# First attention stage of a two-layer network: whole masks behind the products of the maxima, and the maxima's sign on GpSimd

## The chip, the core and the metric

The kernel runs on one core of a Trainium2 chip. A core has a matrix engine (TensorE, PE in the rows; its weight loads are listed apart, as PEld), a vector engine (VectorE, DVE), an activation engine (ScalarE, ACT), GpSimd (POOL), and a queue engine (SyncE, SP) that starts the transfers here. The metric is the time of one execution in microseconds (us), the median of several. Before the change it is 1973.1 us (three runs, 1972.66 to 1973.49).

## The reference, cut to what matters

The network adds four blocks to a residual stream of 4 sequences of 1024 tokens and 128 features. Only the first block is touched. Per sequence and head (16 heads of 8 features, so 64 pairs of head and sequence):

```
q, k, v = (layernorm(x) @ W.T + b) split into 16 heads of 8
sim     = q @ k.T + bias[bucket(i - j)] * SCALE     # bias by distance, per head
sim     = sim - inf where key j > query i           # causal
attn    = softmax(sim);  out = attn @ v
x       = x + out @ Wo.T + bo
```

Later blocks are a tree-routed feed-forward attention, a second attention with 16 heads (unmasked softmax, then masked) and a gated feed-forward layer.

## The kernel before, in words

The stage is `attend_causal`. It has 64 steps, one for each pair of head and sequence, and each engine runs its own list of instructions, written out by hand; semaphores tie the lists together. Queries and keys lie in HBM as three bf16 parts each, from which 48 rows are made (6 pairs of parts by 8 features), loaded twice: into partitions 0 to 47 and 64 to 111. So a product can use the upper or the lower half of TensorE's 128 rows, and products on different halves run side by side. "Half" below always means this half of the rows.

What a step n does:

- **Maxima.** For each block of 128 queries (8 blocks, qb) TensorE makes the causal part of `q k` (128 by (qb+1)·128 elements) in PSUM, as bf16. The blocks are grouped in five tiles, `MAXIMA = [(7,), (0, 6), (1, 5), (2, 4), (3,)]`, called T0 to T4 below, which take turns in two buffers `psM` of two PSUM banks each. The columns of bank 0 come from half 0, those of bank 1 from half 1. The last 128 columns of each block are the diagonal; `mask` (L703) adds minus 1e30 above it with two products of 64 rows each, on the half that wrote them (identity rows times a table). VectorE takes each block's row maxima (L627), then makes minus the maxima as two bf16 parts, high and low (L637, L639).
- **Rows.** One product with an identity (L741, 128 rows, 16 columns) turns these parts into rows; ScalarE copies them (L674) and two transfers put them behind the 48 rows of `qS` (L514), so that a later product also subtracts the maximum.
- **Scores.** Nine units of 512 columns, called u0 to u8 (`PIECES`), each with keys on the partitions; each runs on one half, the two halves in turn, and writes to one of three banks in turn (`psS`). ScalarE takes each with an exponential (L694) to `probs`. u0 waits for the rows' transfer. GpSimd multiplies the columns near the diagonal by the bias factor (L663), eight multiplications a step.
- **Values.** 26 f32 products of `probs` with values and ones (L777, L781), 128 rows by 32 columns, four column groups side by side; each has two records. They come in three parts, `VALUES[0]` to `VALUES[2]`, called V0 to V2.

TensorE's list for a step, with work of three steps in it: u0, u1 of n; T0, T1 of n+2; u2, u3; V0 of n-1; the rows product L741 of n+1; u4; T2; u5, u6; T3; V1; u7, u8; T4; V2. Scores run for n, maxima for n+2, values for n-1.

V0 waits for all eight GpSimd multiplications of step n-1. GpSimd's list is: the eight multiplications of a step, then the copy of the next values (L655).

Of the kernel before, what the change touches and what calls it, by code (L numbers as in the profile page):

```python
# [18 lines left out]
ALU = mybir.AluOpType  # L19
ACT = mybir.ActivationFunctionType  # L20
AXX = mybir.AxisListType.X
# [3 lines left out]
P = 128  # L25
B = 4
# [5 lines left out]
TPB = T // P  # L32
CH = 512
# [23 lines left out]
HALF = 64  # L57
PROWS = PAIRS * HD
# [462 lines left out]
def attend_causal(nc, m, g):  # L521


    NG = HEADS * B
# [4 lines left out]
    ORDER = [0, 1, 2, 3, ROWS, 4, 5, 6, 7, 8]  # L529
    MAXIMA = [(7,), (0, 6), (1, 5), (2, 4), (3,)]  # L530
    NM = len(MAXIMA)
    NEAR_ORDER = [0, 1, 7, 2, 6, 3, 5, 4]
    NEAR_AFTER = [0, 2, 3, 4, 5, 6, 7, 8]
    VALUES = [[(0, 0), (1, 0), (2, 0), (3, 0), (0, 1), (1, 1), (2, 1), (3, 1), (0, 2), (1, 2), (2, 3), (3, 4), (0, 3)],
              [(0, 4), (1, 3), (2, 2), (3, 2), (0, 5), (1, 4)],
              [(0, 6), (1, 5), (2, 4), (3, 3), (0, 7), (1, 6), (2, 5)]]

    ENDS = VALUES[2][-4:]

    def place(kb, qb):  # L540

        for unit, pieces in enumerate(PIECES):
            at = unit * CH
            for of, first, count in pieces:
                if of == kb and first <= qb * P < first + count:
                    return at + qb * P - first
                at += count
        raise AssertionError((kb, qb))

    def near_width(kb):  # L550
# [12 lines left out]
    psO = m.ps("psO", [P, CH])  # L563
    ring = Ring(ORDER, NG, psS)
# [5 lines left out]
    maxima_done, max_taken, block_taken = m.sem("maxima_done"), m.sem("max_taken"), m.sem("block_taken")  # L570
    nm_hi, nm_ready = m.sem("nm_hi"), m.sem("nm_ready")
    slot_done, slot_taken = m.sem("slot_done"), m.sem("slot_taken")
    near_done, v_staged = m.sem("near_done"), m.sem("v_staged")
    pv_done, o_taken = m.sem("pv_done"), m.sem("o_taken")

    with nc.Block() as block:
# [36 lines left out]
        @block.vector  # L613
        def _(dve):
            for u in range(BUFS):
                dve.memset(kS[u][:, :], 1.0).then_inc(cleared, 1)
            for n in range(NG):
                p = n % 2
                for i, blocks in enumerate(MAXIMA):
                    dve.wait_ge(maxima_done, n * NM + i + 1)  # L620
                    at = 0
                    for qb in blocks:
                        if i == 0 and n >= 2:

                            dve.wait_ge(nm_ready, n - 1)
                        w = (qb + 1) * P
                        last = dve.tensor_reduce(mx[:, p, qb:qb + 1], psM[(n * NM + i) % 2][:, at:at + w], AXX, ALU.max)  # L627
                        if qb != blocks[-1]:
                            last.then_inc(block_taken, 1)
                        at += w  # L630
                    last.then_inc(max_taken, 1)
                dve.wait_ge(max_taken, (n + 1) * NM)
                dve.wait_ge(block_taken, (n + 1) * (TPB - NM))
                if n >= 2:

                    dve.wait_ge(slot_done, ring.rows(n - 2) + 1)
                dve.tensor_scalar(nm[:, p, 0, :], mx[:, p, :], -1.0, None, ALU.mult).then_inc(nm_hi, 1)  # L637
                dve.wait_ge(nm_hi, n + 1)
                dve.scalar_tensor_tensor(nm[:, p, 1, :], mx[:, p, :], -1.0, nm[:, p, 0, :], ALU.mult, ALU.subtract).then_inc(nm_ready, 1)  # L639

        @block.gpsimd
        def _(pool):
            for v in v_ones:
                pool.memset(v[:, :, :], 0.0).then_inc(pool_ready, 1)
            pool.wait_ge(pool_ready, len(v_ones))
            for v in v_ones:
                pool.memset(v[:, :, HD:2 * HD], 1.0).then_inc(pool_ready, 1)
            pool.wait_ge(pool_ready, 2 * len(v_ones))

            def stage_v(n):  # L650
                if n >= 3:

                    pool.wait_ge(pv_done, n - 2)
                src = g["v_all"][:, :, :, :].rearrange("p h (b t) e -> p (h b) t e", b=B)[:, n, :, :]
                pool.tensor_copy(v_ones[n % 3][:, :, 0:HD], src).then_inc(v_staged, 1)  # L655

            stage_v(0)
            for n in range(NG):
                pr = probs[n % 2]
                for kb, unit in zip(NEAR_ORDER, NEAR_AFTER):  # L660
                    pool.wait_ge(slot_taken, ring.index(n, unit) + 1)
                    a, w = place(kb, kb), near_width(kb)
                    pool.tensor_tensor(pr[:, a:a + w], pr[:, a:a + w], g["ebias"][:, n // B, 0:w], ALU.mult).then_inc(near_done, 1)  # L663
                if n + 1 < NG:
                    stage_v(n + 1)

# [34 lines left out]
        def _(pe):  # L701
            def mask(out, r, table):

                for s in range(2):
                    done = pe.matmul(out, g["masks"][r:r + HALF, s, 0, :], g["masks"][r:r + HALF, s, table, :], start=False, stop=s == 1)  # L705
                return done

            def maxima(n, i):

                if n >= NG:  # L710
                    return
                u, k = n % BUFS, n * NM + i
                if k >= 2:

                    pe.wait_ge(max_taken, k - 1)
                if i == 0:
                    pe.wait_ge(s_loaded[u], (n // BUFS + 1) * 64)
                ps = psM[k % 2]
                at = 0
                for qb in MAXIMA[i]:  # L720
                    w = (qb + 1) * P
                    for bank in range(2):
                        a, z = max(at, bank * CH), min(at + w, (bank + 1) * CH)
                        if a >= z:
                            continue
                        r, ends = HALF * bank, z == at + w
                        last = pe.matmul(ps[:, a:z], qS[u][r:r + PROWS, qb * P:(qb + 1) * P], kS[u][r:r + PROWS, a - at:z - at], start=True, stop=not ends)  # L727
                        if ends:
                            last = mask(ps[:, z - P:z], r, 1)
                    at += w  # L730
                last.then_inc(maxima_done, 1)

            def rows(n):
# [28 lines left out]
            def values(n, part):  # L762

                if n < 0:
                    return
                if part == 0:
                    pe.wait_ge(v_staged, n + 1)
                    pe.wait_ge(near_done, (n + 1) * TPB)
                    if n > 0:
                        pe.wait_ge(o_taken, n)  # L770
                pr, v = probs[n % 2][:, :], v_ones[n % 3]
                for c, kb in VALUES[part]:
                    out = psO[c * VW:(c + 1) * VW, 0:2 * P]
# [1052 lines left out]
def build(nc, ins, out, phases=99):  # L1826
    ctx = ExitStack()
    with ctx:
# [92 lines left out]
```

## Time and profile before

| | |
|---|---|
| median of three runs | 1973.1 us |
| profiled execution: its time, its span | 1974.91 us, 1973.2 us |
| busy over the whole span: PE, DVE, ACT, POOL | 85%, 80%, 63%, 38% |
| VectorE's maxima in this stage (L627), 512 instructions | 349.7 us |
| GpSimd's multiplications (L663), 512 instructions | 341.6 us |
| ScalarE's exponentials (L694), 576 instructions | 316.4 us |
| TensorE's granted clock in the stage, after its start | 1.00 of full speed |

Busy times are those of the profiled execution. A product's record ends later than its columns have entered, and the next one starts before that, so that TensorE's busy share tells little; the distances between starts tell more. The stage fills about 140 to 560 us of the span.

### The profile page before, as it was taken

To read this page: it belongs to the slowest core of one execution; us is meant where nothing else is said; L and a number is where in the kernel's file an instruction comes from. 1 tells how busy PE (TensorE), PEld (TensorE's weight loads), DVE (VectorE), ACT (ScalarE), POOL (GpSimd) and SP (SyncE) were. 2 spreads that over 40 slices of the span, in tenths; PEclk is the share of its full clock that TensorE was granted. 3 is DMA by queue.
4 is the path that set the end of the run, shared out by engine and by line. 5 is a ranking of instruction groups with operands and counts; after the bars stand their busy time and mean duration, and the time that the engine had idled before them with its cause. 6 is when DMAs were issued, how large, how long until landed. Compare 5 with 4: busy or idle time off the path is not lost. (4 is left out here: it accounts for less than half of the span.)

```text
span 1973.2 us, 48626 instructions
## 1 busy us (share of the span) xinstructions
PE 1671.8 (85%) x19042; PEld 1065.8 (54%) x19066; DVE 1583.8 (80%) x2620; ACT 1240.4 (63%) x2385; POOL 756.6 (38%) x1503
## 2 busy tenths in 40 slices
PE   2529999999955599999999852999999999999935
PEld 1316667676735487877676630444444444444524
DVE  1759999999929699998655566999999999999455
ACT  1427888888841244544433341888899888888825
POOL 0117888888864201000000021444444444444324
PEclk9758999999975599999999875899999999999958
DMA  7352222222222366657100053111111111111031
GB/s 171 112 176 71 85 85 87 85 86 86 80 69 46 38 96 91 95 92 85 25 1 0 1 176 120 47 55 55 55 56 56 56 56 56 56 56 56 16 98 43
DMA packets 131173, 141.86 MB, mean 72 GB/s; under 512 B 22733, under 2 KB 103818, under 8 KB 130954
## 3 DMA queue, kind: packets, MB, share of 16 engines
q1 hardware_dynamic: 117034, 135.50, 27.5%
q10 hardware_dynamic: 13920, 3.36, 1.0%
q8 instruction: 147, 2.41, 0.5%
q14 instruction: 72, 0.59, 0.1%
HBM read 92.70 MB, written 44.98 MB: 70 GB/s over the span
## 5 line engine op out<-in xcount | busy, mean ns | idle before, releaser
L895 DVE TENSOR_REDUCE heads_mx<-heads_psM 128x1 f32<-128x1024 f32 x512 | 602.2, 1220 | 37.7 <-PE heads_psM L984 21.6
L964 ACT ACTIVATE heads_probs<-heads_psS 128x512 f32<-128x512 f32 x1024 | 546.0, 601 | 76.9 <-PE heads_psS L1007 70.8
L663 POOL TENSOR_TENSOR heads_probs<-heads_probs,one_ebias 128x256 f32<-128x256 f32 (+1 forms) x512 | 341.6, 692 | 82.2 <-ACT heads_probs L694 81.9
L933 POOL TENSOR_TENSOR heads_masked<-heads_probs,g_tri 128x128 f32<-128x128 f32 x512 | 233.7, 456 | 359.8 <-ACT heads_probs L964 359.6
L627 DVE TENSOR_REDUCE heads_mx<-heads_psM 128x1 f32<-128x1024 f32 (+7 forms) x512 | 349.7, 750 | 11.0 <-PE heads_psM L705 10.5
L694 ACT ACTIVATE heads_probs<-heads_psS 128x512 f32<-128x512 f32 x576 | 316.4, 603 | 65.9 <-PE heads_psS L705 60.7
L984 PE MATMUL heads_psM<-heads_kS,heads_qS 48*128 48x512 bf16 x1024 | 230.1, 394 | 36.7 <-DMA heads_kS<-k_parts 27.9
L1007 PE MATMUL heads_psS<-heads_qS,heads_kS 50*128 50x512 bf16 x1024 | 237.8, 388 | 0.7 <-ACT heads_probs L964 0.3
L1446 ACT ACTIVATE trees_hid_hi<-trees_hid 128x512 fp32r<-128x512 f32 x192 | 121.6, 634 | 154.0 <-DVE trees_hid L1467 153.2
L727 PE MATMUL heads_psM<-heads_kS,heads_qS 48*128 48x512 bf16 (+3 forms) x768 | 148.0, 336 | 30.2 <-DMA heads_kS<-k_parts 27.4
L1467 DVE SCALAR_TENSOR_TENSOR trees_hid<-trees_psH,g_b,trees_chosen 128x512 f32<-128x512 f32 x192 | 143.9, 750 | 33.5 <-DMA trees_chosen<-leaf_choice 15.8
L1032 PE MATMUL heads_psO<-heads_probs,heads_ones_only 128*32 128x128 f32 x1920 | 161.9, 283 | 0.0
L1033 PE MATMUL heads_psO<-heads_probs,heads_v_ones 128*32 128x128 f32 x1920 | 155.7, 273 | 0.0
L777 PE MATMUL heads_psO<-heads_probs,heads_v_ones 128*32 128x256 f32 x1280 | 151.0, 396 | 2.2 <-POOL heads_probs L663 2.0
L1026 PE MATMUL heads_psO<-heads_probs,heads_ones_only 128*32 128x256 f32 x1280 | 148.7, 390 | 0.0
L755 PE MATMUL heads_psS<-heads_qS,heads_kS 50*128 50x512 bf16 (+3 forms) x768 | 141.5, 334 | 7.4 <-DMA heads_qS<-heads_mrow 5.6
L781 PE MATMUL heads_psO<-heads_probs,heads_v_ones 128*32 128x128 f32 x2048 | 136.6, 279 | 0.0
L1474 DVE SCALAR_TENSOR_TENSOR trees_hid_lo<-trees_hid,trees_hid_hi 128x512 fp32r<-128x512 f32 x192 | 134.1, 699 | 0.1
L1007 PEld LDWEIGHTS heads_psS<-heads_qS,heads_kS 50*128 50x128 bf16 x1024 | 69.7, 93 | 114.0 <-ACT heads_probs L964 54.7
L1026 PE MATMUL heads_psO<-heads_probs,heads_v_ones 128*32 128x256 f32 x768 | 120.9, 394 | 0.0
L984 PEld LDWEIGHTS heads_psM<-heads_kS,heads_qS 48*128 48x128 bf16 x1024 | 56.5, 95 | 112.5 <-DVE heads_mx L895 64.5
L1032 PEld LDWEIGHTS heads_psO<-heads_probs,heads_ones_only 128*32 128x32 f32 x1920 | 72.7, 108 | 82.1 <-issue 82.0
(238 smaller groups left out, 3180.2 us busy)
## 6 DMA issues: line engine op xcount, KB each, us to landing
heads_qS<-q_parts SPq DMA_DIRECT2D x256, 96.0 KB
heads_kS<-k_parts SPq DMA_DIRECT2D x256, 96.0 KB
trees_chosen<-leaf_choice SPq DMA_DIRECT2D x96, 256.0 KB
head_outputs<-heads_oT SPq DMA_DIRECT2D x128, 128.0 KB
q_parts<-proj_parts SPq DMA_DIRECT2D x16, 384.0 KB, 2.6
k_parts<-proj_parts SPq DMA_DIRECT2D x16, 384.0 KB, 3.3
q_parts<-proj_parts SPq DMA_DIRECT2D x16, 256.0 KB, 3.5
k_parts<-proj_parts SPq DMA_DIRECT2D x16, 256.0 KB, 3.6
```

The lines of the kernel that those rows point to most:

```text
L627: last = dve.tensor_reduce(mx[:, p, qb:qb + 1], psM[(n * NM + i) % 2][:, at:at + w], AXX, ALU.max)
L663: pool.tensor_tensor(pr[:, a:a + w], pr[:, a:a + w], g["ebias"][:, n // B, 0:w], ALU.mult).then_inc(near_done, 1)
L694: act.activation(probs[n % 2][:, slot * CH:(slot + 1) * CH], ring.bank(i)[:, :], ACT.Exp).then_inc(slot_taken, 1)
L777: last = pe.matmul(out.rearrange("p (q w) -> p q w", w=P), v[:, kb, :], bass.AP(pr.tensor, a, [list(pr.ap[0]), [far - a, 2], [1, P]]), sta ...
L895: dve.tensor_reduce(mx[:, n % 2, k:k + 1], psM[k % 2][:, :], AXX, ALU.max, negate=True).then_inc(max_taken, 1)
L933: pool.tensor_tensor(masked[n % 2][:, kb, :], probs[n % 2][:, kb, kb * P:(kb + 1) * P], g["tri"][:, 0:P], ALU.mult).then_inc(near_done, 1)
L964: act.activation(probs[n % 2][:, kb, h * CH:(h + 1) * CH], ring.bank(i)[:, :], ACT.Exp).then_inc(slot_taken, 1)
L984: last = pe.matmul(psM[k % 2][:, h * CH:(h + 1) * CH], qS[u][r:r + PROWS, k * P:(k + 1) * P], kS[u][r:r + PROWS, h * CH:(h + 1) * CH], sta ...
L1007: pe.matmul(ring.bank(i)[:, :], kS[u][r:r + RROWS, kb * P:(kb + 1) * P], qS[u][r:r + RROWS, h * CH:(h + 1) * CH], start=True, stop=True).t ...
L1026: pe.matmul(out.rearrange("p (q w) -> p q w", w=P), v_ones[v][:, kb, :] if kb < c else ones_only[:, :], both, start=kb == 0, stop=False, t ...
L1032: pe.matmul(out[:, 0:P], ones_only[:, :], pr[:, c, :], start=False, stop=False, tile_position=(0, c * VW))
L1033: pe.matmul(out[:, P:2 * P], v_ones[v][:, kb, :], pr[:, b, :], start=False, stop=False, tile_position=(0, c * VW))
```

## The change

Five edits, all in `attend_causal`:

1. A tile of maxima issues its products for the two banks in turn (half 0, half 1, ...), and behind all of them one mask product for each block, over all 128 rows and 128 columns, where two products of 64 rows stood behind each block's own.
2. VectorE's maxima are written with their sign turned (`negate=True`); its two small instructions on them are gone.
3. GpSimd makes the two bf16 parts of step n+1 ahead of step n's multiplications (a copy to bf16, and a difference that waits for it).
4. V0 waits for four multiplications of its step, V1 for all eight.
5. The values are dealt out anew: V0 has 9 products and not 13, V1 has 10 and not 6, V2 the same 7. The list `NEARS` has the blocks in the order that they had.

```diff
-    NEAR_ORDER = [0, 1, 7, 2, 6, 3, 5, 4]
-    NEAR_AFTER = [0, 2, 3, 4, 5, 6, 7, 8]
-    VALUES = [[(0, 0), (1, 0), (2, 0), (3, 0), (0, 1), (1, 1), (2, 1), (3, 1), (0, 2), (1, 2), (2, 3), (3, 4), (0, 3)],
...
+    NEARS = [((0,), 0), ((1,), 2), ((7,), 3), ((2,), 4), ((6,), 5), ((3,), 6), ((5,), 7), ((4,), 8)]
+    NEAR_FIRST = 4
+    VALUES = [[(0, 0), (1, 0), (2, 0), (3, 0), (0, 1), (1, 1), (2, 1), (3, 1), (0, 2)],
...
-                        last = dve.tensor_reduce(mx[:, p, qb:qb + 1], psM[(n * NM + i) % 2][:, at:at + w], AXX, ALU.max)
+                        last = dve.tensor_reduce(mx[:, p, qb:qb + 1], psM[(n * NM + i) % 2][:, at:at + w], AXX, ALU.max, negate=True)
...
-                dve.tensor_scalar(nm[:, p, 0, :], mx[:, p, :], -1.0, None, ALU.mult).then_inc(nm_hi, 1)
-                dve.wait_ge(nm_hi, n + 1)
-                dve.scalar_tensor_tensor(nm[:, p, 1, :], mx[:, p, :], -1.0, nm[:, p, 0, :], ALU.mult, ALU.subtract).then_inc(nm_ready, 1)
...
+            def minus_maxima(n):
+
+                p = n % 2
+                pool.wait_ge(max_taken, (n + 1) * NM)
+                pool.wait_ge(block_taken, (n + 1) * (TPB - NM))
+                if n >= 2:
+                    pool.wait_ge(slot_done, ring.rows(n - 2) + 1)
+                pool.tensor_copy(nm[:, p, 0, :], mx[:, p, :]).then_inc(nm_hi, 1)
+                pool.wait_ge(nm_hi, n + 1)
+                pool.tensor_tensor(nm[:, p, 1, :], mx[:, p, :], nm[:, p, 0, :], ALU.subtract).then_inc(nm_ready, 1)
...
+            minus_maxima(0)
             for n in range(NG):
-                pr = probs[n % 2]
-                for kb, unit in zip(NEAR_ORDER, NEAR_AFTER):
+                if n + 1 < NG:
+                    minus_maxima(n + 1)
+                for blocks, unit in NEARS:
...
-                at = 0
+                runs, ends, at = ([], []), [], 0
                 for qb in MAXIMA[i]:
                     w = (qb + 1) * P
                     for bank in range(2):
                         a, z = max(at, bank * CH), min(at + w, (bank + 1) * CH)
...
-                        last = pe.matmul(ps[:, a:z], qS[u][r:r + PROWS, qb * P:(qb + 1) * P], kS[u][r:r + PROWS, a - at:z - at], start=True, stop=not ends)
-                        if ends:
-                            last = mask(ps[:, z - P:z], r, 1)
+                        if a < z:
+                            runs[bank].append((qb, a, z, a - at))
                     at += w
+                    ends.append(at)
+                for j in range(max(len(of) for of in runs)):
+                    for bank in range(2):
+                        if j < len(runs[bank]):
+                            qb, a, z, first = runs[bank][j]
...
+                for z in ends:
+                    later = [e for e in ends if z < e <= -(-z // CH) * CH]
+                    last = pe.matmul(ps[:, z - P:z], g["identb"][:, :], g["masks"][:, 0, 1, :], start=False, stop=not later)
                 last.then_inc(maxima_done, 1)
...
-                    pe.wait_ge(near_done, (n + 1) * TPB)
+                    pe.wait_ge(near_done, n * len(NEARS) + NEAR_FIRST)
...
+                if part == 1:
+                    pe.wait_ge(near_done, (n + 1) * len(NEARS))
```

On TensorE, from T0 of step n+2 to the first score unit behind T1. The name `heads_psM` is the maxima's buffer, `heads_psS` the scores'. Before:

```order
L727 MATMUL heads_psM<-heads_kS,heads_qS 128x512 x2
L705 MATMUL heads_psM<-g_masks 128x128 x2
L727 MATMUL heads_psM<-heads_kS,heads_qS 128x128
L705 MATMUL heads_psM<-g_masks 128x128 x2
L727 MATMUL heads_psM<-heads_kS,heads_qS 128x384
L727 MATMUL heads_psM<-heads_kS,heads_qS 128x512
L705 MATMUL heads_psM<-g_masks 128x128 x2
L755 MATMUL heads_psS<-heads_qS,heads_kS 128x512
```

and now (L750 is the whole mask, over 128 rows; L746 and L775 are the old L727 and L755):

```order
L746 MATMUL heads_psM<-heads_kS,heads_qS 128x512 x2
L750 MATMUL heads_psM<-g_masks,g_identb 128x128
L746 MATMUL heads_psM<-heads_kS,heads_qS 128x128
L746 MATMUL heads_psM<-heads_kS,heads_qS 128x512
L746 MATMUL heads_psM<-heads_kS,heads_qS 128x384
L750 MATMUL heads_psM<-g_masks,g_identb 128x128 x2
L775 MATMUL heads_psS<-heads_qS,heads_kS 128x512
```

Six mask products on halves became three whole ones, and T1's product of 384 columns moved behind that of 512.

On TensorE, V0 and the rows product behind it, up to u4's product (`heads_psO` is the values' buffer). Before:

```order
L777 MATMUL heads_psO<-heads_probs,heads_v_ones 32x256 x4
L781 MATMUL heads_psO<-heads_probs,heads_v_ones 32x128
L777 MATMUL heads_psO<-heads_probs,heads_v_ones 32x256 x3
L781 MATMUL heads_psO<-heads_probs,heads_v_ones 32x128 x5
L741 MATMUL heads_psS<-g_identb,heads_nm 16x128
L755 MATMUL heads_psS<-heads_qS,heads_kS 128x512
```

and now (L799 and L803 are the old L777 and L781, L761 the old L741):

```order
L799 MATMUL heads_psO<-heads_probs,heads_v_ones 32x256 x4
L803 MATMUL heads_psO<-heads_probs,heads_v_ones 32x128
L799 MATMUL heads_psO<-heads_probs,heads_v_ones 32x256 x3
L803 MATMUL heads_psO<-heads_probs,heads_v_ones 32x128
L761 MATMUL heads_psS<-g_identb,heads_nm 16x128
L775 MATMUL heads_psS<-heads_qS,heads_kS 128x512
```

Four products of 128 columns, one for each column group, left V0; V1 has them now.

On GpSimd, one step from the copy of the values on. Before:

```order
L655 COPY heads_v_ones<-one_v_all 128x8x8
L663 TENSOR_TENSOR heads_probs<-heads_probs,one_ebias 128x256 x2
L663 TENSOR_TENSOR heads_probs<-heads_probs,one_ebias 128x128
L663 TENSOR_TENSOR heads_probs<-heads_probs,one_ebias 128x256 x5
L655 COPY heads_v_ones<-one_v_all 128x8x8
```

and now:

```order
L647 COPY heads_v_ones<-one_v_all 128x8x8
L656 CAST heads_nm<-heads_mx 128x8
L658 TENSOR_TENSOR heads_nm<-heads_mx,heads_nm 128x8
L667 TENSOR_TENSOR heads_probs<-heads_probs,one_ebias 128x256 x2
L667 TENSOR_TENSOR heads_probs<-heads_probs,one_ebias 128x128
L667 TENSOR_TENSOR heads_probs<-heads_probs,one_ebias 128x256 x5
```

The two small instructions of the maxima stand between the copy and the multiplications.

## Rows read from the trace of the kernel before

**Rows 1.** Stretch: us, busy PE, PEld, DVE, ACT, POOL, clock, DMA share, GB/s.

```profile
350.00:450.00 100.00, 98.92 (x1711) 70.24 (x1710) 97.80 (x157) 84.11 (x173) 85.90 (x142) 1.00 0.28 86
```

**Rows 2.** Waits, 150 to 560 us: waiter, releaser: us in total, times, longest.

```profile
PEld heads_psS L755 <- DMA heads_qS<-heads_mrow: 15.9, 40, 1.1
DVE heads_mx L627 <- PE heads_psM L705: 7.8, 20, 1.4
```

**Rows 3.** Timeline of TensorE, one step: start us, us, line, tiles, xcount [idle before].

```profile
176.22 0.22 PE L741 MATMUL heads_psS<-g_identb,heads_nm 128*16 128x128 bf16 x1
...
176.71 0.40 PE L727 MATMUL heads_psM<-heads_kS,heads_qS 48*128 48x256 bf16 x2
...
177.06 0.40 PE L755 MATMUL heads_psS<-heads_qS,heads_kS 50*128 50x256 bf16 x3
...
177.41 0.40 PE L727 MATMUL heads_psM<-heads_kS,heads_qS 48*128 48x384 bf16 x2
...
177.85 0.30 PE L781 MATMUL heads_psO<-heads_probs,heads_v_ones 128*32 128x128 f32 x2
...
178.20 0.28 PE L781 MATMUL heads_psO<-heads_probs,heads_v_ones 128*32 128x128 f32 x2
178.42 0.40 PE L755 MATMUL heads_psS<-heads_qS,heads_kS 50*128 50x128 bf16 x3
...
178.78 0.38 PE L727 MATMUL heads_psM<-heads_kS,heads_qS 48*128 48x512 bf16 x1
179.00 0.27 PE L705 MATMUL heads_psM<-g_masks 64*128 64x128 bf16 x2
179.20 0.31 PE L781 MATMUL heads_psO<-heads_probs,heads_v_ones 128*32 128x128 f32 x3
...
179.77 0.40 PE L755 MATMUL heads_psS<-heads_qS,heads_kS 50*128 50x512 bf16 x2
...
181.39 0.64 PE L777 MATMUL heads_psO<-heads_probs,heads_v_ones 128*32 128x256 f32 x8
...
182.50 0.22 PE L741 MATMUL heads_psS<-g_identb,heads_nm 128*16 128x128 bf16 x1
182.65 0.39 PE L755 MATMUL heads_psS<-heads_qS,heads_kS 50*128 50x512 bf16 x1
```

**Rows 4.** All rows products from 169 to 552 us: ns min/median/max, first and last start.

```profile
L741 PE MATMUL heads_psS<-g_identb,heads_nm x60: 218/219/220, 169.4 to 547.7; 128*16 128x128 bf16 x60
```

**Rows 5.** Timeline of TensorE: rows products, and u0, of three later steps.

```profile
304.44 0.22 PE L741 MATMUL heads_psS<-g_identb,heads_nm 128*16 128x128 bf16 x1
...
308.63 0.40 PE L755 MATMUL heads_psS<-heads_qS,heads_kS 50*128 50x512 bf16 x2 [0.58 <-DMA heads_qS<-heads_mrow]
...
311.37 0.22 PE L741 MATMUL heads_psS<-g_identb,heads_nm 128*16 128x128 bf16 x1
...
317.65 0.22 PE L741 MATMUL heads_psS<-g_identb,heads_nm 128*16 128x128 bf16 x1
```

**Rows 6.** Timeline of VectorE, the same steps.

```profile
302.32 0.69 DVE L637 TENSOR_SCALAR heads_nm<-heads_mx 128x8 bf16<-128x8 f32 x1
...
303.13 5.44 DVE L627 TENSOR_REDUCE heads_mx<-heads_psM 128x1 f32<-128x1024 f32 x8
...
312.42 1.29 DVE L627 TENSOR_REDUCE heads_mx<-heads_psM 128x1 f32<-128x256 f32 x2 [0.49 <-PE heads_psM L705]
```

**Rows 7.** Timeline of TensorE's weight loads, where V0 begins.

```profile
303.33 0.14 PEld L777 LDWEIGHTS heads_psO<-heads_probs,heads_v_ones 128*32 128x32 f32 x5
```

**Rows 8.** Timeline of GpSimd: this stage, then the second attention's maxima.

```profile
302.93 0.24 POOL L655 COPY heads_v_ones<-one_v_all 128x64 f32<-128x64 f32 x1
...
305.80 3.47 POOL L663 TENSOR_TENSOR heads_probs<-heads_probs,one_ebias 128x256 f32<-128x256 f32 x5 [0.49 <-ACT heads_probs L694]
...
1229.41 0.19 POOL L914 CAST heads_nm<-heads_mx 128x8 bf16<-128x8 f32 x1 [10.12 <-DVE heads_mx L895]
1229.68 0.20 POOL L916 TENSOR_TENSOR heads_nm<-heads_mx,heads_nm 128x8 bf16<-128x8 f32 x1
```

More of the change, by code:

```diff
@@ L531, in attend_causal @@
     NM = len(MAXIMA)
-    NEAR_ORDER = [0, 1, 7, 2, 6, 3, 5, 4]
-    NEAR_AFTER = [0, 2, 3, 4, 5, 6, 7, 8]
-    VALUES = [[(0, 0), (1, 0), (2, 0), (3, 0), (0, 1), (1, 1), (2, 1), (3, 1), (0, 2), (1, 2), (2, 3), (3, 4), (0, 3)],
-              [(0, 4), (1, 3), (2, 2), (3, 2), (0, 5), (1, 4)],
-              [(0, 6), (1, 5), (2, 4), (3, 3), (0, 7), (1, 6), (2, 5)]]
-    ENDS = VALUES[2][-4:]
+    NEARS = [((0,), 0), ((1,), 2), ((7,), 3), ((2,), 4), ((6,), 5), ((3,), 6), ((5,), 7), ((4,), 8)]
+    NEAR_FIRST = 4
+    VALUES = [[(0, 0), (1, 0), (2, 0), (3, 0), (0, 1), (1, 1), (2, 1), (3, 1), (0, 2)],
+              [(1, 2), (2, 2), (3, 2), (0, 3), (1, 3), (2, 3), (3, 4), (0, 4), (1, 4), (0, 5)],
+              [(2, 4), (3, 3), (0, 6), (1, 5), (2, 5), (0, 7), (1, 6)]]
+    ENDS = [(3, 3), (2, 5), (0, 7), (1, 6)]
     def place(kb, qb):
@@ L631, in _ @@
                     last.then_inc(max_taken, 1)
[L632 to L636, printed above, removed]
-                dve.tensor_scalar(nm[:, p, 0, :], mx[:, p, :], -1.0, None, ALU.mult).then_inc(nm_hi, 1)
-                dve.wait_ge(nm_hi, n + 1)
-                dve.scalar_tensor_tensor(nm[:, p, 1, :], mx[:, p, :], -1.0, nm[:, p, 0, :], ALU.mult, ALU.subtract).then_inc(nm_ready, 1)
         @block.gpsimd
@@ L655, in stage_v, with weight @@
                 pool.tensor_copy(v_ones[n % 3][:, :, 0:HD], src).then_inc(v_staged, 1)
+            def minus_maxima(n):
[7 more added lines that the diff above has]
+                pool.tensor_tensor(nm[:, p, 1, :], mx[:, p, :], nm[:, p, 0, :], ALU.subtract).then_inc(nm_ready, 1)
+            def weight(n, blocks):
+                pr, eb, w = probs[n % 2][:, :], g["ebias"][:, n // B, :], near_width(blocks[0])
+                a = place(blocks[0], blocks[0])
+                step = place(blocks[-1], blocks[-1]) - a
+                at = bass.AP(pr.tensor, a, [list(pr.ap[0]), [step, len(blocks)], [1, w]])
+                by = bass.AP(eb.tensor, eb.offset, [list(eb.ap[0]), [0, len(blocks)], [1, w]])
+                pool.tensor_tensor(at, at, by, ALU.mult).then_inc(near_done, 1)
             stage_v(0)
+            minus_maxima(0)
             for n in range(NG):
-                pr = probs[n % 2]
-                for kb, unit in zip(NEAR_ORDER, NEAR_AFTER):
+                if n + 1 < NG:
+                    minus_maxima(n + 1)
+                for blocks, unit in NEARS:
                     pool.wait_ge(slot_taken, ring.index(n, unit) + 1)
-                    a, w = place(kb, kb), near_width(kb)
-                    pool.tensor_tensor(pr[:, a:a + w], pr[:, a:a + w], g["ebias"][:, n // B, 0:w], ALU.mult).then_inc(near_done, 1)
+                    weight(n, blocks)
                 if n + 1 < NG:
@@ L723, in maxima @@
                         a, z = max(at, bank * CH), min(at + w, (bank + 1) * CH)
-                        if a >= z:
-                            continue
-                        r, ends = HALF * bank, z == at + w
-                        last = pe.matmul(ps[:, a:z], qS[u][r:r + PROWS, qb * P:(qb + 1) * P], kS[u][r:r + PROWS, a - at:z - at], start=True, stop=not ends)
-                        if ends:
-                            last = mask(ps[:, z - P:z], r, 1)
-                    at += w
+                        if a < z:
+                            runs[bank].append((qb, a, z, a - at))
+                    at += w
+                    ends.append(at)
[3 more added lines that the diff above has]
+                            qb, a, z, first = runs[bank][j]
+                            r = HALF * bank
+                            pe.matmul(ps[:, a:z], qS[u][r:r + PROWS, qb * P:(qb + 1) * P], kS[u][r:r + PROWS, first:first + z - a],
+                                      start=j == 0, stop=j + 1 == len(runs[bank]) and (bank + 1) * CH not in [-(-e // CH) * CH for e in ends])
+                for z in ends:
+                    later = [e for e in ends if z < e <= -(-z // CH) * CH]
+                    last = pe.matmul(ps[:, z - P:z], g["identb"][:, :], g["masks"][:, 0, 1, :], start=False, stop=not later)
                 last.then_inc(maxima_done, 1)
```

## The prediction, made before the result

> **What bounds the kernel now.** First the stretches [rows 1]: in the stage TensorE (98.9 of 100 us) and VectorE (97.8) are both nearly full at a granted clock of 1.00, ScalarE and GpSimd are not. The shares don't say which of the two sets the pace, and the change helps one and touches the other. Then the waits [rows 2]: no wait of TensorE for VectorE is among the large ones. VectorE waits for TensorE 20 times (7.8 us), and u0's weight loads wait 40 times for the transfer of the maxima's rows.
>
> Then one step on TensorE [rows 3], from one rows product to the next, 6.28 us. Its stretches: u0 to V0 1.62 (179.77 to 181.39), V0 to the product behind the rows product 1.26 (to 182.65), from there to V1 1.48 (177.85 less 176.22 less 0.15), V1 to u7 0.57, u7 to V2 0.78, V2 to u0 0.57. Sum 6.28. There is no hole in it beyond those where halves and whole rows change (below).
>
> VectorE needs about the same: 0.81 us for its two small instructions (302.32 to 303.13) and 5.44 for the maxima, 6.25 [rows 6]. To tell them apart I take a step in which VectorE has time over. u0 waited for its rows until 308.63 and the step took 311.37 - 304.44 = 6.93 us [rows 5]; in the next one VectorE stood still for 0.49 us waiting for a maxima tile [rows 6], so it was not the bound; yet the step took 317.65 - 311.37 = 6.28 us again [rows 5]. So TensorE's own list sets the step at 6.28, plus what u0 waits for the rows. From 169.4 to 547.7 us there are 59 distances [rows 4], 6.41 us in the mean: 0.13 a step, 7.8 us in all, is that wait.
>
> **The change part by part.**
>
> *VectorE.* 0.81 us a step goes from an engine that doesn't set the pace: worth nothing. The sign in the maxima's instruction is taken at nothing; 0.8 us a step of new slack covers it. If VectorE were the bound, this would be the gain (a rival below).
>
> *GpSimd.* It gets two small instructions. The second attention stage has the same pair: 1229.41 to 1229.68 plus 0.20, so 0.47 us [rows 8]. They queue behind the step's last multiplication and the copy, which ends at 302.93 + 0.24 = 303.17; both parts are then ready at 303.64, and the rows product stood at 304.44 [rows 5]: 0.8 us of cover. Behind them the first multiplication moves by 0.47, into 0.49 us of idle time before the long run of five [rows 8], and V1, not V0, now waits for all eight, 3 us later. GpSimd's step becomes about 85.9/100 x 6.4 + 0.47 = 6.0 us [rows 1], under TensorE's. So nothing; if the pair took over 0.8 us more than there, the excess would be paid every step.
>
> *Values.* V0 loses 128 columns a column group, V1 gains them. V0 has 640 and lasts 1.11 us (181.39 to 182.50) [rows 3], so 128 are 0.22 us: -0.22 ahead of the rows product, +0.22 behind it. The step's sum doesn't change, but the rows leave earlier.
>
> *Masks.* This decides. Prices from rows: 512 columns on a half take 0.22 us (178.78 to 179.00), two mask products 0.055 each (0.27 for two records against 0.22 for one) [rows 3]. And a **switch** between products on halves and products over all rows: the second mask of T4 starts at 179.055, its columns are in at 179.11, V2 starts at 179.20, so 0.09 us pass. The way back: 182.50 + 0.055 to 182.65, so 0.10; and the last f32 columns of V1 (178.20, 0.11 for 128 columns) end at 178.31, u7 starts at 178.42, 0.10 too. In a switch the weights aren't loaded ahead: V0's load starts at 303.33 with its product [rows 7].
>
> Before, all maxima and scores ran on halves, and a step had three switches in and three out. Now each of five tiles ends over all rows. That adds for T0, T1, T2 one in (0.09) and one out (0.10) each; for T3 and T4 the way in is there before, and one more change, whole bf16 of 128 columns to f32 of 32 columns, comes behind the mask. No row shows that one; by both neighbours I take 0.09. The stretches anew:
> - u0 to V0: u0 0.34 (a unit of 512 and two masks is 0.22 + 0.11), T0 0.22, in 0.09, mask 0.055, out 0.10, T1 0.22, in 0.09, two masks 0.11, out 0.10, u2 beside u3 0.34, in 0.09: 1.755, was 1.62. **+0.135**. Without the four new switches it would be 1.375: the 1.62 is not all TensorE's work, since u3 waits for ScalarE to take u0's bank, and that hides a part.
> - T2: 0.35 (176.71 to 177.06), now 0.22 + 0.09 + 0.115 + 0.10 = 0.525. **+0.17**
> - T3 with its way in: 0.44 (177.41 to 177.85), now 0.22 + 0.09 + 0.115 + 0.09 = 0.515. **+0.075**
> - T4: 0.42 (178.78 to 179.20), now 0.22 + 0.09 + 0.055 + 0.09 = 0.455. **+0.035**
>
> Together +0.415 us: a step of 6.70. The products in turn on both halves give little back: T1 and T2 kept both halves busy to about the same end before.
>
> A rule speaks for this price beyond the rows. The Trainium skill, in "TensorEngine Tiling (Array Packing)", Key Properties, has it that a change of tiling mode, not of the tile alone, drains the engine. By this rule the unseen change behind T3 and T4 isn't free either; for halves against 32-column products the trace agrees, with its 0.09 and 0.10.
>
> *What the transfer gives back.* From the rows product to u0 the way was 3.55 us (176.22 to 179.77). It gets longer by T2, T3, V1 and T4: 0.17 + 0.075 + 0.22 + 0.035 = 0.50. The rows' transfer starts at the same place, so each wait shrinks by 0.50. The one at 308.63 was 4.19 - 3.55 = 0.64 [rows 5], 0.14 would be left; most of the 7.8 us goes, I keep 1. That is -7.
>
> **Sum.** 62 of 64 steps hold maxima tiles of step n+2. 62 x 0.415 = +25.7, less 7: +19 us. The profiled execution's own time is 1974.9, which becomes about 1994; it stands 1.8 above the median of 1973.1, so the median becomes 1992.
>
> The unseen size is a switch with 128 columns of weights. Nearest rows: 0.09 and 0.10, the latter with weights of 128 columns on a half. From below nothing excludes 0 for a bf16 product; from above, a whole load behind the drain (V0's five loads took 0.14 in all [rows 7]). Each 0.01 us moves the result by 8 x 62 x 0.01 = 5 us. I take the nearest rows.
>
> **Rivals.**
>
> *The switch is free for whole masks* (the other side). Place: T0 to T4, and the point that decides is a switch of 0.04 us. At 0, the first stretch stays at 1.62, T2, T3 and T4 lose about 0.09 together: -6 us; the way from rows to u0 grows by 0.13, which takes some 3 us from the waits: 1964. For it: a mask's load in the same mode does hide, since two masks start 0.055 apart [rows 3]. Against: every change of mode in rows 3 costs 0.09 to 0.10. The Trainium skill's page "TensorE: Matmul & The Clock Gate", under Step-by-step: what each phase is for, states that a weight load is pulled ahead of running products if it goes to the background buffer; by that the switch would cost nothing and this rival would hold. Rows 7 show no such load at a switch.
>
> *VectorE set the pace after all.* Then the step would fall to GpSimd's 6.0: 62 x (6.41 - 6.0) = 25 us, 1948. For it: 97.8% busy. Against: the step of 6.28 after VectorE had idled.
>
> *A switch costs more with whole weights*, 0.14: 62 x 8 x 0.045 = +22 more, 2014. For it: the load of 128 rows and columns may stand in the open. Against: the way out to u4 has 128 columns too, at 0.10.
>
> *The maxima's parts come late from GpSimd*, behind multiplications: the rows product would wait by what exceeds 0.8 us; with 0.2 over, +12, 2004. For it: GpSimd's list is nearly full. Against: the cover above, which grows as the step gets longer.
>
> **How the numbers follow.** The forecast, 0.78: 1992, its own range 1980 to 2003. Free or nearly free switches 0.09 (faster; 0.02 of it lands within 0.2%). VectorE's pace 0.03 (faster). Dearer switches 0.07 and late parts 0.03 (slower). About 0.2%, 4 us, is what can be told from no change. The forecast's own lower edge gives 0.02 to no change. So slower 0.86, faster 0.10, same 0.04. The range of 8 in 10 takes a switch from 0.06 to 0.12: 1977 to 2007.
>
> **What would show it.** In the profile after: rows products 6.70 us apart (61 distances), with hardly a wait of u0 for its transfer; 0.09 us ahead of each whole mask and as much behind; 1.75 us from u0 to V0; V0 to the rows product 0.89; VectorE's busy share near 5.44/6.70 = 81%, now waiting for TensorE in every step; GpSimd near 6.0/6.7. I am wrong if whole masks start within 0.03 us behind the halves' columns, if steps fall under 6.28, or if the rows product waits for GpSimd.

## The result, and the profile after

The change makes the kernel slower: 1997.5 us median of 4 runs (1995.03 to 1999.07) against 1972.9 (1971.57 to 1973.49), a ratio of 1.0125 [1.0107, 1.0142]. The prediction was 1992 us and slower. In the profiled executions the span went from 1973.2 to 1995.0 us, +21.8.

The windows of the kernel after, in the columns of [rows 1]:

```profile
150.00:250.00 100.00, 99.01 (x1314) 54.81 (x1313) 78.81 (x113) 72.85 (x147) 78.28 (x148) 0.89 0.24 73
350.00:450.00 100.00, 100.00 (x1503) 58.47 (x1499) 82.90 (x120) 80.22 (x163) 86.48 (x162) 1.00 0.26 80
```

In the middle of the stage TensorE no longer stands still at all, VectorE fell from 97.8 to 82.9 (81 predicted), and GpSimd took its two instructions without becoming full. The first row matters for the clock: in the same 100 us the kernel before had

```profile
150.00:250.00 100.00, 97.37 (x1582) 67.91 (x1580) 94.97 (x153) 79.26 (x162) 80.35 (x132) 0.93 0.26 80
```

a mean granted clock of 0.93, not 0.89.

The waits of the kernel after, 150 to 590 us, answer to [rows 2]:

```profile
ACT heads_probs L707 <- PE heads_psS L718: 93.4, 253, 4.5
DVE heads_mx L627 <- PE heads_psM L750: 77.6, 127, 2.7
PEld heads_psM L750 <- issue: 75.2, 312, 0.5
```

ScalarE and VectorE now wait for TensorE, VectorE twice a step. Of the wait for the rows' transfer (14.8 us before, 176 to 540 us) one record of 0.2 us is left in the same stretch. The new third row is the change itself: 312 times the weight loads of a whole mask (L750) stood idle for want of nothing that the profile shows, 0.24 us in the mean. They come at the changes between halves and whole rows.

One step on TensorE after, for [rows 3] (L761 rows product, L775 scores, L746 maxima, L750 whole masks, L718 the scores' masks on halves, L799 and L803 values):

```profile
303.63 0.22 PE L761 MATMUL heads_psS<-g_identb,heads_nm 128*16 128x128 bf16 x1
303.78 0.39 PE L775 MATMUL heads_psS<-heads_qS,heads_kS 50*128 50x512 bf16 x1
303.79 0.39 PE L746 MATMUL heads_psM<-heads_kS,heads_qS 48*128 48x512 bf16 x1
304.01 0.27 PE L718 MATMUL heads_psS<-g_masks 64*128 64x128 bf16 x2
304.12 0.38 PE L746 MATMUL heads_psM<-heads_kS,heads_qS 48*128 48x256 bf16 x2
304.43 0.29 PE L750 MATMUL heads_psM<-g_masks,g_identb 128*128 128x128 bf16 x2
304.65 0.40 PE L775 MATMUL heads_psS<-heads_qS,heads_kS 50*128 50x256 bf16 x3
...
305.32 0.28 PE L750 MATMUL heads_psM<-g_masks,g_identb 128*128 128x128 bf16 x2
305.53 0.30 PE L803 MATMUL heads_psO<-heads_probs,heads_v_ones 128*32 128x128 f32 x1
...
306.33 0.40 PE L775 MATMUL heads_psS<-heads_qS,heads_kS 50*128 50x128 bf16 x3
306.56 0.28 PE L718 MATMUL heads_psS<-g_masks 64*128 64x128 bf16 x4
306.68 0.38 PE L746 MATMUL heads_psM<-heads_kS,heads_qS 48*128 48x512 bf16 x1
306.99 0.23 PE L750 MATMUL heads_psM<-g_masks,g_identb 128*128 128x128 bf16 x1
307.15 0.30 PE L803 MATMUL heads_psO<-heads_probs,heads_v_ones 128*32 128x128 f32 x1
...
307.73 0.40 PE L775 MATMUL heads_psS<-heads_qS,heads_kS 50*128 50x512 bf16 x2
...
309.52 0.64 PE L799 MATMUL heads_psO<-heads_probs,heads_v_ones 128*32 128x256 f32 x8
...
310.41 0.22 PE L761 MATMUL heads_psS<-g_identb,heads_nm 128*16 128x128 bf16 x1
```

| stretch, us | before | predicted | after |
|---|---|---|---|
| u0 to V0 | 1.62 | 1.755 | 1.79 |
| V0 to rows product | 1.11 | 0.89 | 0.89 |
| rows product to V1 | 1.63 | 1.875 | 1.90 |
| V1 to u7 | 0.57 | 0.79 | 0.80 |
| u7 to V2 | 0.78 | 0.815 | 0.82 |
| V2 to u0 | 0.57 | 0.57 | 0.58 |
| step | 6.28 | 6.70 | 6.78 |

A whole mask shows both prices in one place. Behind T4, the 512 columns start at 306.68, so that they are in at 306.90 (a group of 512 takes 0.22, [rows 3]); the mask starts at 306.99, is in at 307.05, and V2 starts at 307.15: 0.09 in, 0.10 out. Two whole masks start about 0.065 us apart (0.29 for two records, 0.22 or 0.23 for one), halves 0.055.

The account of the span's +21.8 (rounded terms): 63 distances of the stage at +0.50 a step are +31.5; the waits for the transfer that went, 0.13 a step over 59, are -7.8; the start of the stage +3.9; its end -4.2; the rest of the kernel -1.6. This compares one profiled execution of each kernel.

Of the start's 3.9, 1.1 lie ahead of the first rows product (145.9 and 147.0 us; in the other kernels run it stands between 145.4 and 148.5), and 2.7 in the first three distances, 27.8 us together against 23.5, where three times 0.50 were counted already. The third of them runs mostly at the lower of the clock's two levels after (granted 0.50 of full speed from 165 to 170 us), and at the higher one before (1.00).

The end of the stage is a term that the prediction did not have. Before, V0 of the last step waited 2.03 us for the last of eight multiplications of GpSimd:

```profile
566.28 1.08 PE L777 MATMUL heads_psO<-heads_probs,heads_v_ones 128*32 128x256 f32 x8 [2.03 <-POOL heads_probs L663]
```

After, it wants four of them and waits 0.85 us, for ScalarE:

```profile
590.82 0.42 PE L799 MATMUL heads_psO<-heads_probs,heads_v_ones 128*32 128x256 f32 x4 [0.85 <-ACT heads_oT L693]
```

That is 1.2 us of the 4.2. Most of the rest is the clock. From the last rows product to the last product of the values 15.6 us pass before and 11.4 after, and the granted clock in them, in the columns of [rows 1], is (two rows of before, one of after)

```profile
560.00:562.00 2.00, 2.00 (x26) 1.38 (x19) 0.00 (x0) 0.00 (x0) 0.81 (x2) 0.50 0.22 68
566.00:570.00 4.00, 3.61 (x52) 2.89 (x52) 0.00 (x0) 0.03 (x1) 0.18 (x1) 0.59 0.11 33
590.00:594.00 4.00, 2.37 (x52) 1.70 (x52) 0.00 (x0) 1.06 (x3) 1.91 (x3) 1.00 0.11 33
```

TensorE was busy 4.30 of the 5 us ahead of the first fall (554 to 559 us) and 0.25 of the 2 us ahead of the second. e8 below keeps the old V0, waits the same 2.03 us, has the clock at 1.00 to the end and takes 12.8 us. So the new values are worth 1.4 us at the end where the clock stays up; that they also keep it up isn't shown (it fell in three of the four kernels with the wait: before, e1 and e4).

### The profile page after: what moved, and what is told of

The parts are those of the page before. It is cut to its first block and busy times, and to the rows that moved or that the text cites. A ratio compares the mean times of both kernels' runs of the same rounds, so it can differ in the third digit from the quotient of the medians.

```text
span 1995.0 us, 47626 instructions
## 1 busy us (share of the span) xinstructions
PE 1704.5 (85%) x18554; PEld 1029.0 (52%) x18554; DVE 1542.5 (77%) x2492; ACT 1244.8 (62%) x2385; POOL 781.3 (39%) x1631
## 5 line engine op out<-in xcount | busy, mean ns | idle before, releaser
L627 DVE TENSOR_REDUCE heads_mx<-heads_psM 128x1 f32<-128x1024 f32 (+7 forms) x512 | 358.0, 752 | 82.0 <-PE heads_psM L750 80.9
L667 POOL TENSOR_TENSOR heads_probs<-heads_probs,one_ebias 128x256 f32<-128x256 f32 (+1 forms) x512 | 346.3, 693 | 57.7 <-ACT heads_probs L707 44.9
L746 PE MATMUL heads_psM<-heads_kS,heads_qS 48*128 48x512 bf16 (+3 forms) x768 | 154.5, 337 | 29.3 <-DMA heads_kS<-k_parts 27.3
L799 PE MATMUL heads_psO<-heads_probs,heads_v_ones 128*32 128x256 f32 x1280 | 149.5, 391 | 0.9 <-ACT heads_oT L693 0.9
L803 PE MATMUL heads_psO<-heads_probs,heads_v_ones 128*32 128x128 f32 x2048 | 135.7, 278 | 0.1
L775 PE MATMUL heads_psS<-heads_qS,heads_kS 50*128 50x512 bf16 (+3 forms) x768 | 129.8, 336 | 1.2 <-ACT heads_probs L707 1.1
L1582 POOL COPY wide_qs<-two_qkT 128x1024 f32 (+1 forms) x4 | 4.2, 1039 | 284.2 <-SPq L1526 179.5
L396 POOL TENSOR_TENSOR proj_rest<-proj_qk,proj_parts 128x1024 f32<-128x1024 f32 x16 | 34.0, 2124 | 207.6 <-ACT proj_parts L428 207.6
```

What stands on the lines that cost most here:

```text
L667: pool.tensor_tensor(at, at, by, ALU.mult).then_inc(near_done, 1)
```

## The experiments

Twelve kernels were run, and the kernel before beside them each time: 1975.3 us beside e1 to e4, 1972.3 beside e5 to e8, 1975.1 beside e9 to e12. The ratios are to these runs. Theory M: the masks' switches carry the whole loss. Against it: the loss comes from the maxima's order, from GpSimd, or from the dealing of the values.

**e1: whole masks alone.** The kernel before with the new `maxima` (products in turn, masks whole and behind) and nothing else.

```diff
+                for z in ends:
+                    last = pe.matmul(ps[:, z - P:z], g["identb"][:, :], g["masks"][:, 0, 1, :], start=False, stop=not later)
```

> The kernel before, with the maxima's products and whole masks of the change and nothing else of it (VectorE keeps its two small instructions, GpSimd and the values are as before). Theory M (TensorE's own list sets the step, and the whole masks' switches make it longer): the step goes from 6.28 to 6.78 us as in the changed kernel, but the way from the rows product to u0 grows by only 0.32 us instead of 0.5, so some 2 us of the waits for the rows' transfer stay: about 1999 us (1995 to 2003), slower by 1.1 to 1.5%. Rival G (the loss comes from GpSimd's two small instructions or from the values dealt out anew): about 1973 us, as before. A rival by which VectorE's relief paid for part of the masks' price would give well over 2005 us here.

1999.2 us, 1.0119 [1.0104, 1.0135]: as slow as the whole change. All rows products of e1, 176 to 540 us, in the columns of [rows 4]:

```profile
L748 PE MATMUL heads_psS<-g_identb,heads_nm x54: 218/219/220, 178.7 to 537.7; 128*16 128x128 bf16 x54
```

359.0 us in 53 distances, a step of 6.77.

**e2: all but the masks.** The kernel after with the old `maxima`.

> The changed kernel with the maxima's products and masks put back as they were (two mask products of 64 rows behind each block); the sign, the pair on GpSimd, the values and the waits stay changed. Theory M: the step falls back to 6.28 us, u0 comes 0.22 us later behind the rows product, so the waits for the transfer shrink by about 4 us, and the stage's end starts its values earlier (2 to 4 us): 1965 to 1969 us. Rival V (VectorE set the pace before, 0.81 us a step is freed): a step of about 6.0 us, 1945 to 1952 us. Rival G: 1990 us or more.

1968.2 us, 0.996 [0.9946, 0.9973]. The shortest step is 6.29, as before; the mean comes from the same row of e2,

```profile
L754 PE MATMUL heads_psS<-g_identb,heads_nm x58: 218/219/220, 175.8 to 538.7; 128*16 128x128 bf16 x58
```

362.9 us in 57 distances, 6.37. e1 and e2 together settle theory M: the masks take it all, and what is left of the change is worth 7 to 8 us when the masks stay on halves. With whole masks it is worth nothing that can be told (e1 is as slow as the whole change): part of its gain is less waiting for the transfer (a mean step of 6.37 against 6.41), and e1's step of 6.77 hardly waits for it any more (0.6 us, 176 to 540 us).

**e3: the new order with masks on halves.** The mask stays behind the products, but as two products of 64 rows:

```diff
-                    last = pe.matmul(ps[:, z - P:z], g["identb"][:, :], g["masks"][:, 0, 1, :], start=False, stop=not later)
+                    last = mask(ps[:, z - P:z], HALF * ((z - 1) // CH), 1)
```

> The changed kernel with its order of a tile (products of the two halves in turn, masks behind all of them), but each mask as two products of 64 rows on the half that wrote the columns. Theory M: no switch is added, each half has the same columns as before, so a step of 6.28 us and 1965 to 1969 us, the same as with the old order of the masks. Rival B (putting the masks behind the products is what costs, whole or not): 1990 to 1997 us.

1966.6 us, 0.9953 [0.9939, 0.9966]; step 6.24 at the shortest. So the order of the products isn't the loss either; it gives 0.04 us a step (6.28 were expected). Without a switch the next units start inside T2:

```profile
302.43 0.27 PE L718 MATMUL heads_psS<-g_masks 64*128 64x128 bf16 x2
302.54 0.27 PE L746 MATMUL heads_psM<-heads_kS,heads_qS 48*128 48x256 bf16 x1
302.55 0.28 PE L718 MATMUL heads_psM<-g_masks 64*128 64x128 bf16 x2
...
302.67 0.27 PE L774 MATMUL heads_psS<-heads_qS,heads_kS 50*128 50x256 bf16 x1
```

(TensorE's timeline of e3.) u5 starts at 302.67 between two masks of T2; in the kernel after it had to wait for both whole ones (304.43, then 304.65).

**e4: the sign alone.** The kernel before with `negate=True`, and the two small instructions on GpSimd.

> The kernel before, with only the sign taken by VectorE's maxima and the two small instructions moved to GpSimd ahead of the next multiplications. VectorE needs 0.81 us less a step. Theory M: 1973 us within 2, the step stays 6.28 us. Rival V: 1945 to 1952 us. Rival G (the maxima's parts come late from GpSimd, V0 waits for multiplications that moved back by 0.47 us): each step pays up to 0.4 us, 1980 to 1998 us.

1974.9 us, 1.000 [0.9988, 1.0012]. VectorE got its 0.8 us a step and spends them waiting, as its timeline shows:

```profile
304.14 2.42 DVE L627 TENSOR_REDUCE heads_mx<-heads_psM 128x1 f32<-128x1024 f32 x3 [0.29 <-PE heads_psM L711]
307.06 1.29 DVE L627 TENSOR_REDUCE heads_mx<-heads_psM 128x1 f32<-128x256 f32 x2 [0.49 <-PE heads_psM L711]
```

An engine busy 97.8% was not the bound. V0's wait of 2.02 us at the stage's end is still there in this kernel.

**e5: whole masks for T3 and T4 only.** e2 with the whole mask `if i >= 3:`.

> The kernel e2 (all of the change but its masks), with whole masks behind the products in T3 and T4 alone, the two tiles behind which values follow. Theory M: only two switches a step are added (in, ahead of the mask, stood there before the values already; new is the one from the mask to the values), so the step gets longer by the changed kernel's T3 and T4 alone: 0.08 + 0.05 = 0.13 us, 62 times, 8 us over e2: 1976 us (1973 to 1979). If a whole mask costs the same wherever it stands (a fifth of the 31 us each), it would be 12 us over e2: 1980 us.

1975.1 us, 1.0018 [1.0009, 1.0027]; step 6.43, +0.14 over e2's 6.29. These two tiles had the switch to whole rows before; what they add is the change nobody could see before, from a whole bf16 product to 32-column f32. It isn't free. T0 to T2 carry the rest, 6.78 - 6.43 = 0.35.

**e6: the values alone.** The new `VALUES`, V0 behind four multiplications, V1 behind eight.

> The kernel before with only edits 4 and 5: the values dealt out anew, V0 waiting for four multiplications and V1 for all. Theory M: step 6.28 us, the waits for the rows' transfer shrink by up to 0.22 us each (4 us) and the end of the stage gains 2 to 4 us: 1966 to 1970 us where the kernel before has 1975. If e2's gain came from VectorE's or GpSimd's part instead, this one shows none: 1975 us.

1965.3 us, 0.9967 [0.9955, 0.9979]. Two terms: the mean step is 6.35 (6.41 before), 59 x 0.06 = 3.5 us, and the end of the stage, from the last rows product on, takes 11.4 us, as in the kernel after (1.4 to 4.2 us less than with the old V0, by the clock). The waits for the transfer, 176 to 540 us, fell from 14.8 us in 38 to

```profile
PEld heads_psS L755 <- DMA heads_qS<-heads_mrow: 9.2, 29, 0.8
```

**e7: no masks on the maxima, the rest of the change kept.** e2, and

```diff
-                        r, ends = HALF * bank, z == at + w
+                        r, ends = HALF * bank, False
...
-                act.activation(mrow[n % 2][:, :], ring.bank(ring.rows(n))[0:SHIFTS * TPB, 0:P], ACT.Copy).then_inc(slot_taken, 1)
+                act.activation(mrow[n % 2][:, :], ring.bank(ring.rows(n))[0:SHIFTS * TPB, 0:P], ACT.Copy, bias=30.0).then_inc(slot_taken, 1)
```

It leaves the masks off the maxima (not off the scores): the maximum that the softmax subtracts then takes in keys behind the query, and 60 is added back (30 on each of its two rows), so that nothing vanishes; both cancel in the quotient. e8 does the same.

> The kernel e2 without any mask on the maxima: the maximum of a diagonal block then takes in keys behind the query, which only enlarges the number that the softmax subtracts; so that nothing vanishes, 60 is added back (30 on each of the two rows of the maximum, as the bias of ScalarE's copy), which cancels in the softmax. TensorE loses 16 mask products a step. Theory M: TensorE's list falls to about 5.93 us, VectorE needs 5.47, GpSimd about 5.95 to 6.0: the step is about 6.0 us, the waits for the transfer stay: 1950 to 1957 us. If the values' and scores' waits for ScalarE hold the step at 6.28, it shows 1968 us.

1960.9 us, 0.9949 [0.9936, 0.9962], the fastest of all. The shortest step is 5.90, near the 5.93 expected, but the mean is 6.25,

```profile
L754 PE MATMUL heads_psS<-g_identb,heads_nm x58: 219/219/314, 181.4 to 537.5; 128*16 128x128 bf16 x58
```

and the time missed its range by 4 us. The waits of e7, 176 to 540 us:

```profile
DVE heads_mx L627 <- PE heads_psM L740: 40.5, 95, 2.0
PEld heads_psS L768 <- DMA heads_qS<-heads_mrow: 27.5, 43, 2.1
```

A shorter step leaves less time between the rows product and u0, and the waits for the transfer (14.8 us in the kernel before) take back more than half of what the list gave.

**e8: no masks, the sign left on VectorE.** The kernel before with the same two edits.

> The kernel before without the masks on the maxima (and 60 added back as in e7): TensorE's list is short, VectorE still has its two small instructions and GpSimd has no more to do than before. Theory M with VectorE as the next bound: TensorE's list would allow 5.93 us, but VectorE needs 6.25: the step is 6.25 to 6.28 us and the waits for the transfer vanish in TensorE's slack: 1966 to 1970 us, some 12 us above e7. If VectorE's 0.81 us were never on the path, e8 would be as fast as e7.

1967.9 us, 0.9982 [0.9973, 0.9992]. The time is in its range, but not as expected: the shortest step is 6.02, the mean 6.36, and the waits for the transfer, which were to vanish, grew. Here VectorE also holds TensorE up (95.55 of 100 us busy, 350 to 450 us):

```profile
PEld heads_psS L755 <- DMA heads_qS<-heads_mrow: 25.7, 51, 2.0
PEld heads_psM L727 <- DVE heads_mx L627: 24.5, 71, 0.5
```

TensorE's loads wait for VectorE 71 times (waits, 176 to 540 us), a row that [rows 2] don't have. In e7 TensorE's waits for VectorE are 7.7 us in 28. With the masks, moving the sign is worth nothing (e4). What it is worth without them isn't shown: e7 is 7 us faster than e8, but it also has the new values, which alone brought 7 us in e6.

**e9 to e12: the rows product ahead of V0**, to give the transfer V0's 0.9 to 1.1 us more. The edit of all four:

```diff
+                rows(n + 1)
                 values(n - 1, 0)
-                rows(n + 1)
```

in e6 with e3's masks (e9), in e6 (e10), in e7 (e11, where GpSimd's copy of the values also goes behind the maxima's parts) and in e3 (e12, likewise).

> The kernel before with the values dealt out anew (as e6), the masks on halves behind the products (as e3), and the rows product ahead of V0 and not behind it. Theory M with the rows' transfer as the second term: the rows product comes 0.9 us earlier against u0, so no wait for the transfer is left; TensorE's list is 6.24 to 6.25 us, VectorE, which keeps its pair, needs 6.25: a step of 6.25 to 6.28 us, 1959 to 1962 us. If the waits are not the transfer's latency but the queue's load, they stay: 1963 to 1966 us.

> e6 with the rows product ahead of V0 and nothing else. In e6 the maxima's parts are ready 0.3 us before V0 starts, so the rows product doesn't wait for them; e6's 3.5 us of waits for the rows' transfer go, the step stays 6.29: 1961 to 1963 us. If the waits stay: 1965 us.

> e7 (no masks on the maxima, sign and pair moved) with the rows product ahead of V0, and GpSimd's pair ahead of its copy of the values. e7's steps are 5.90 us without a wait but 6.24 in the mean, by the waits for the rows' transfer. Theory M: these go; the rows product now waits up to 0.1 to 0.2 us for GpSimd, whose own step is 5.95 to 6.0: steps of about 6.0 us, 1944 to 1950 us. If GpSimd's late parts cost more than the transfer's waits, 1960 us or more.

> e3 (all of the change, but masks on halves) with the rows product ahead of V0, and GpSimd's pair ahead of its copy. e3's steps are 6.24 us without a wait, 6.34 in the mean. Theory M: the waits for the transfer go (5.7 us); the maxima's parts, ready 0.24 us after V0's start in e3, come about 0.2 us earlier, so the rows product waits 0.05 us or less: 1960 to 1963 us, the same as e9. If GpSimd's pair stays late, each step pays 0.2 us and nothing is gained: 1967 us or more.

All four missed: e9 took 1992.6 us, 1.0089 [1.0068, 1.0109]; e10 1993.4, 1.0103 [1.0082, 1.0123]; e11 1973.0, 0.9991 [0.9979, 1.0004]; e12 1994.1, 1.0103 [1.0082, 1.0123]. The transfer's wait did vanish in e9, e10 and e12, and fell to 4.1 us in e11 (176 to 540 us); in e10's waits, 170 to 560 us:

```profile
PE heads_psS L741 <- ACT heads_probs L694: 20.1, 57, 0.4
PEld heads_psS L755 <- DMA heads_qS<-heads_mrow: 0.3, 1, 0.3
```

The first row is new, one in every step. Its place, TensorE's timeline of e10 and then ScalarE's:

```profile
303.75 0.27 PE L705 MATMUL heads_psS<-g_masks 64*128 64x128 bf16 x2
304.38 0.22 PE L741 MATMUL heads_psS<-g_identb,heads_nm 128*16 128x128 bf16 x1 [0.35 <-ACT heads_probs L694]
304.50 0.64 PE L779 MATMUL heads_psO<-heads_probs,heads_v_ones 128*32 128x256 f32 x8
```

```profile
303.63 1.58 ACT L694 ACTIVATE heads_probs<-heads_psS 128x512 f32<-128x512 f32 x3
305.06 0.25 ACT L674 ACTIVATE heads_mrow<-heads_psS 16x128 bf16<-16x128 f32 x1
```

The rows product writes into the ring of score banks, and its bank must be emptied by the exponential of an earlier unit (u1). V0's work had covered that. The 0.35 us is counted from the end of the last mask's record. By starts, u0 to the rows product takes 2.05 us where u0 to V0 takes 1.62 in e6, and the rows product and V0, up to u4, take 1.13 where V0 and the rows product take 1.05. Together that is the step: 6.80 against e6's 6.29. e9, e11 and e12 show the same idle 0.35 us in every step. My expectations had followed the transfer alone and left out the bank.

## Why the prediction came out as it did

**The bound.** Right. TensorE's list sets the step: e4 took 0.8 us a step off VectorE and changed nothing. The rival of VectorE's pace fell with it. In e8, where the list would allow less, TensorE's loads do wait for VectorE. The reading of the stretch from u0 to V0, that ScalarE and not TensorE's work makes it 1.62, holds too: e7 took its six mask products away and it is still 1.62 us, with u3 starting 0.05 us behind the end of u0's exponential as in the kernel before.

**The switch.** Right in kind, in place and nearly in size: 0.09 to 0.10 us each way with whole masks, where the rows of before gave 0.09 and 0.10 for neighbours. The rival of free switches and the one of 0.14 both fell in the kernel after. The rule that a change of mode drains the engine (the Trainium skill, "TensorEngine Tiling (Array Packing)", Key Properties) agrees with the trace here as well, for the third kind of change too (0.10 from T4's mask to V2, and e5's step). The rule of a load pulled ahead into the background buffer (the Trainium skill, "TensorE: Matmul & The Clock Gate", Step-by-step: what each phase is for) does not show at a switch: the rival that rested on it gave 1964 us for the kernel after, which took 1997.5.

**The step, +0.50 and not +0.415.** This is the term that was mis-sized. I took 0.09 for a way in, 0.10 for a way out to halves and 0.09 for the unseen one. In the step shown they are 0.09 to 0.10, 0.10 to 0.11, and 0.09 and 0.10; two masks start 0.065 apart and not 0.055. Each is off by 0.01 or less, and all the same way. Over the 62 steps the 0.085 make 5.3 us, and the stage has one distance more, 0.5.

**The waits.** -7 predicted, with 1 of 7.8 left; -7.8 in the account: they went wholly.

**GpSimd's pair.** Right: at nothing. In the timeline of after

```profile
308.89 0.24 POOL L647 COPY heads_v_ones<-one_v_all 128x64 f32<-128x64 f32 x1
309.06 0.19 POOL L656 CAST heads_nm<-heads_mx 128x8 bf16<-128x8 f32 x1
309.34 0.20 POOL L658 TENSOR_TENSOR heads_nm<-heads_mx,heads_nm 128x8 bf16<-128x8 f32 x1
309.50 1.93 POOL L667 TENSOR_TENSOR heads_probs<-heads_probs,one_ebias 128x256 f32<-128x256 f32 x3
```

both parts are ready at 309.54, and the rows product stands at 310.41: 0.87 us of cover, 0.8 predicted.

**The values.** Neutral for the step, as predicted; but the edit also shortens V0's wait at the stage's end, 1.2 us that I had not looked for: I read steps of the middle only. The other 3 us of the end (mostly the clock, which fell there in the profiled execution of before), and the +3.9 at the start, were not in the prediction either. That these missing terms (+3.9, -4.2, -1.6) come to no more than -1.9, and against the step's 5.8, is luck.

**The sum.** The profiled own time became 1996.7, where 1994 was predicted (1993.6 unrounded): 5.8 of the step, 3.9 of the start, -0.8 of the waits, -4.2 of the end, -1.6 elsewhere. The other 2.6 us of the distance to 1997.5 come from the choice of one execution: the profiled one of before lay 1.8 above its median, the one of after 0.8 below.

What stays open: why the granted clock rises later at the stage's start (0.89 and 0.93 in the windows above). e1 to e12 were not made for it. Whole masks alone don't explain it: from 160 to 165 us the clock is still 0.50 in e1, e5 and in the kernel after, but also in e9, which has no whole mask, and 0.69 in the kernel before.

## What to carry to other kernels

Count the changes of mode on TensorE before counting its products: here 16 mask products became 8, and the eight added changes cost more than the saved ones brought, 0.50 us of a step of 6.28. Keep work of one mode together, or keep a mask in the mode of the products that it follows; e3 shows that its place behind them is harmless. And before taking time from a full engine, look for a step in which it idled and see whether the step got shorter; before moving a product forward, list all that it waits for, the bank it writes included. Of the versions run, e7 beats both kernels by the most (-10 to -11 us against the kernel before), and with the masks kept e6 and e3 do (-7 and -9).

## What the runs showed of the hardware that was not expected

- Products for the free half start ahead of some that stand before them in the order. In the kernel after, T2's 512 columns start at 303.79, and u4's two masks, which are written before them, at 304.01.
- A tiny VectorE instruction can wait, within its own record, for one of GpSimd's multiplications to end. In the kernel before, at the stage's start with GpSimd idle, the 128x8 instruction of [rows 6] took 0.17 us and not 0.69:

```profile
145.46 0.17 DVE L637 TENSOR_SCALAR heads_nm<-heads_mx 128x8 bf16<-128x8 f32 x1
```

The one of 0.69 ends at 302.32 + 0.69 = 303.01, and the run of multiplications beside it (299.52 and 3.47 us long) ends at 302.99. All 63 long ones of that kernel end 0.03 us behind the end of a multiplication.

- In e8 one step has its pair at 0.17 and 0.62 us, the next at 0.68 and 0.17: which of the two is long changes with where the multiplications end beside them. This was read, not tried by itself.
- A transfer that a step waits for takes back what the list gives. Taking 0.38 us from TensorE's list (6.28 to 5.90, e7) shortened the mean step by 0.16 (6.41 to 6.25).
